# First-layer experts on gathered token blocks, with the second attention's first key stacks loaded in the same stage

## The chip, the cores and the metric

The kernel runs on one core of a Trainium2 chip. The metric is the device time of one execution in microseconds (us). Engines are named as in the profile: PE (TensorE matmul), PEld (its weight loads), DVE (VectorE), ACT (ScalarE), POOL (GpSimd), SP (SyncE, which here only issues DMAs; its rows are called SPq).

## The reference, cut to what matters

Four sequences of 256 tokens (1024 tokens, width 256) pass two layers, each a cross-attention and a mixture of experts. The change lies in the experts of the first layer, and touches what stands beside them. What they compute, for all 1024 rows `x` after a layer norm:

```python
topk_indices, topk_weights = _router(x, router_weight, e_bias)      # 2 of 16 experts per token
combine = zeros((T, 16)).at[arange(T)[:, None], topk_indices].add(topk_weights)
h1 = einsum('th,ehi->tei', x, w_up)                                 # 256 -> 128 per expert
a = relu2(h1) * combine[:, :, None]                                 # relu, squared
routed = einsum('tei,eih->th', a, w_down)                           # 128 -> 256
shared = relu2(x @ shared_up) @ shared_down                         # 256 -> 512 -> 256, all tokens
return routed + shared
```

The second attention has 16 heads of 16 over the same context; its queries come from the rows that this stage leaves, its keys only from the context.

## The kernel before

The program is a row of stages, and all engines meet between them: first attention (`prep_l0`, `attention` with `L0`), the first experts (`route_and_experts_l0`), the second attention (`load_first_units`, `attention` with `L1`), and the second layer's router, shared expert and routed experts (`route_shared_l1`, `routed_l1`). Tokens lie in 8 tiles of 128 rows; a half is 4 tiles. Every engine runs its own list of instructions in program order, and semaphores join them.

In `route_and_experts_l0` PE transposes the normed rows into `xT`, projects them on the router, and then runs the shared expert in 8 units (`hidden`, `outputs`), with one tile of the second attention's values (`values`) behind each. ACT rectifies a unit's hidden rows, POOL squares them (line 1131). Meanwhile DVE picks each token's two experts and writes the weights of all 16 to `comb` (lines 1256 to 1289).

The routed experts follow as a dense loop of 32 units `n` (16 experts times two halves): `routed_hidden(n)` multiplies an expert's up weights with all 512 rows of the half (line 1041), ACT rectifies, POOL squares (line 1141), `routed_outputs(n)` gives four tiles of outputs (line 1052), and DVE adds each to `xs`, times its weight, which is zero for most rows (line 1392). Expert weights (256 KB each) come through four slots of `f_w`, each loaded by SP when its unit is done (line 1427). Behind unit `n` each engine runs `keys(n)` and `queries(n)`: the second attention's keys, their norm and their split into three bf16 parts, and from unit 16 on the same for the queries of the first half, since `xs` of that half is then finished. SP writes the parts to the stacks in memory (`written`, line 233), and between its loads also fetches the second layer's first 12 experts (`load_weights`, line 1760).

The second attention begins with `load_first_units`: SP loads the key and query stacks of four units (line 469), keys first; the first scores (line 629) wait for both of unit 0. `LateQueries` makes the queries of the second half in that stage.

Of the kernel before, what the change touches and what calls it, by code (L numbers as in the profile page):

```python
# [210 lines left out]
KEYS_WRITTEN = (20, 21, 23, 24)  # L211
SPLIT_BANKS = (6, 7, 0, 1)
# [24 lines left out]
def prep_l0(nc, m, io, block, ctx):  # L237
# [158 lines left out]
    def _(pool):  # L396
        load_ones(pool, m, io, lay, m.ks0)
        nc.gpsimd.memset(m.v1[:], 0.0)
# [93 lines left out]
def attention(nc, m, lay, io, block, w_dram, b_dram, v_bias=None, late=None):  # L492
# [18 lines left out]
    with ExitStack() as ctx:  # L511
# [38 lines left out]
        def _(sp):  # L550
# [9 lines left out]
            for u in range(U):  # L560
                shift_rows(u, u % NBUF)
                if u == 0 and lay is L0:
                    for k in (4, 5):
                        load_side(sp, m, lay, ks, "k", loaded, k, k)
                        load_side(sp, m, lay, qs, "q", loaded, k, k)
                if u == 1 and late is not None:
# [345 lines left out]
WSLOTS = 4  # L912
GRP, GSZ = 4, 4


def route_and_experts_l0(nc, m, io):

    with ExitStack() as ctx:
# [3 lines left out]
        def sb(n, shape, dt=F32):  # L922
# [9 lines left out]
        hot, den = sb("hot", [2, NT, E0]), sb("den", [NT])  # L932
        ld, step, root_in, root_out, xn_ready, xt_ps, xt_ready, logit_ps, score_ready = (sem(n) for n in (
# [5 lines left out]
        UNITS0 = 2 * E0  # L939
        qh_xn, qh_turned, qh_copied, qh_ps, qh_cent, qh_squared, qh_summed, qh_scaled = (sem("qh_" + n) for n in (  # L940
            "xn", "turned", "copied", "ps", "cent", "squared", "summed", "scaled"))
        erelu, ehid = sb("erelu", [2, HT]), sb("ehid", [2, HT])
        e_up_ps, e_relu_done, e_hid_done, e_down_ps, e_added, comb_ready = (sem(n) for n in (
            "e_up_ps", "e_relu_done", "e_hid_done", "e_down_ps", "e_added", "comb_ready"))
        s_loaded = [sem(f"s_loaded{e}") for e in range(SH0)]
# [3 lines left out]
        hvar, hwork, sq = sb("hvar", [NT, H]), sb("hwork", [4, NT * H]), sb("sq", [2, D])  # L949
# [11 lines left out]
        def _(sp):  # L961
# [3 lines left out]
            sp.dma_start(later[:], io["later"].partition_broadcast(P)).then_inc(ld, 16)  # L965
            for e in range(SH0):
                sp.dma_start(sup[:, e, :, :].rearrange("p c n -> p (c n)"), io["L0_w"][E0 + e, :, 0:KD * I0]
                             ).then_inc(s_loaded[e], 16)
                sp.dma_start(sdown[:, e, :], io["L0_w"][E0 + e, :, KD * I0:KD * I0 + D]).then_inc(s_loaded[e], 16)
            for j in range(WSLOTS):  # L970
                load_expert_l0(sp, m, io, j, j)
# [20 lines left out]
        def _(pe):  # L992
# [106 lines left out]
            for n in range(UNITS0):  # L1099
                if n + 1 < UNITS0:  # L1100
                    routed_hidden(n + 1)
# [1374 lines left out]
```

## Time and profile before

| | us |
|---|---|
| median of 3 runs (lowest to highest) | 764.84 (762.67 to 765.81) |
| the profiled execution's own time | 768.52 |
| its span, first to last instruction | 766.6 |
| first experts' stage, to the first row of the next | 194.06 to 370.18 |
| of it the dense loop on PE | 244.37 to 368.05 |
| PE busy over the span | 646.2 (84%) |

The durations below are of the profiled execution, which lies 3.68 us above the median. Busy shares are means over stages with different limits, so each stage is read by itself: which engine is full there, and what ended the waits of the others. A matmul's record is longer than its place in the pipeline, so the cost of a matmul is read from where the next one starts.

### The profile page before, as it was taken

How to read it: one execution, taken by the hardware profiler on the slowest of the kernel's cores; microseconds unless marked ns; L12 is line 12 of the kernel's file. 1: busy time of each engine (PE TensorE's matmuls, PEld its weight loads, DVE VectorE, ACT ScalarE, POOL GpSimd, SP SyncE). 2: the span in 40 equal slices, each digit the busy share in tenths (PEclk: the TensorE clock that was granted, in tenths of full speed). 3: DMA queues.
4: the chain of work that ended last, by engine and by line, in shares of the span. 5: the costliest groups of instructions: out<-in, count | busy, mean ns of one | idle time of the engine just before them, and what ended most of it. 6: DMA issues, size and time to landing. Idle time of an engine off the chain costs nothing. (4 is left out here: it accounts for less than half of the span.)

```text
span 766.6 us, 12462 instructions
## 1 busy us (share of the span) xinstructions
PE 646.2 (84%) x4224; PEld 388.7 (51%) x4224; DVE 425.9 (56%) x1130; ACT 297.3 (39%) x552; POOL 259.2 (34%) x403
## 2 busy tenths in 40 slices
PE   1657988887799999999569999599999999999750
PEld 1542444444566666676335556365666555555330
DVE  4668788863330767967687564448982222222116
ACT  1332777785323122423036667342214232232110
POOL 5350011111135323313101333302258677777140
PEclk9895899998599999999779999759999999999875
DMA  3086122100600464553914310099001899999907
GB/s 116 1 277 197 45 64 64 45 2 1 175 0 1 127 182 151 166 179 97 240 32 126 85 45 2 12 276 245 4 12 36 236 290 276 271 269 279 266 32 274
DMA packets 82615, 99.59 MB, mean 130 GB/s; under 512 B 11610, under 2 KB 58049, under 8 KB 82547
## 3 DMA queue, kind: packets, MB, share of 16 engines
q1 hardware_dynamic: 74738, 86.53, 39.9%
q0 software_dynamic: 5600, 8.53, 4.3%
q10 hardware_dynamic: 2208, 3.67, 1.3%
q8 instruction: 36, 0.59, 0.3%
q14 instruction: 33, 0.26, 0.1%
HBM read 82.42 MB, written 21.63 MB: 136 GB/s over the span
## 5 line engine op out<-in xcount | busy, mean ns | idle before, releaser
L769 DVE TENSOR_REDUCE l_mx<-ps 128x2 f32<-128x512 f32 (+2 forms) x256 | 125.9, 550 | 46.7 <-PE ps L629 46.4
L857 ACT ACTIVATE l_prob<-ps 128x1024 f32<-128x1024 f32 x96 | 98.4, 1026 | 27.0 <-PE ps L659 26.8
L629 PE MATMUL ps<-l_ks,l_qs 48*128 48x256 bf16 (+1 forms) x384 | 73.1, 305 | 26.4 <-DMA l_qs<-l_q_stacks 13.2
L1392 DVE SCALAR_TENSOR_TENSOR xs<-ps,comb,xs 128x256 f32<-128x256 f32 x128 | 55.8, 482 | 59.5 <-PE ps L1052 59.4
L674 PE MATMUL ps<-l_prob,v 128*9 128x256 f32 (+1 forms) x768 | 71.4, 395 | 1.1 <-ACT l_prob L857 1.1
L2146 POOL DMA_INDIRECT y_rows<-r_sw,row x53 | 53.4, 1008 | 44.3 <-DVE r_sw L2287 33.6
L2280 DVE TENSOR_TENSOR r_hot<-r_hot,ps 128x352 f32<-128x352 f32 (+1 forms) x35 | 15.1, 432 | 95.1 <-ACT r_hot L2255 95.1
L1141 POOL TENSOR_TENSOR r_ehid<-r_erelu 128x512 f32<-128x512 f32 x32 | 35.5, 1109 | 83.6 <-ACT r_erelu L1245 83.5
L1790 POOL DMA_INDIRECT xg<-x_rows,r_empty x53 | 56.2, 1060 | 19.9 <-issue 10.5
L1052 PE MATMUL ps<-f_w,r_ehid 128*128 128x256 f32 x256 | 60.8, 381 | 0.2
L1041 PE MATMUL ps<-xT,f_w 128*128 128x512 f32 x128 | 60.0, 593 | 0.0
L629 PEld LDWEIGHTS ps<-l_ks,l_qs 48*128 48x128 bf16 (+1 forms) x384 | 30.1, 103 | 58.0 <-issue 21.8
L1052 PEld LDWEIGHTS ps<-f_w,r_ehid 128*128 128x128 f32 x256 | 48.5, 190 | 21.0 <-issue 13.9
L659 PE MATMUL ps<-l_qs,l_ks 50*128 50x256 bf16 (+1 forms) x384 | 57.6, 285 | 0.0
L597 POOL TENSOR_TENSOR attn<-rest,l_rec 128x32 f32<-128x32 f32 x64 | 14.4, 246 | 115.0 <-DVE l_rec L788 115.0
L597 POOL TENSOR_TENSOR l_ctxv<-rest,l_rec 128x64 f32<-128x64 f32 x64 | 17.6, 296 | 84.6 <-DVE l_rec L788 84.6
L2255 ACT ACTIVATE r_hot<-ps 128x352 f32<-128x352 f32 (+1 forms) x35 | 13.7, 392 | 79.8 <-PE ps L2184 79.8
L1874 PE MATMUL ps<-xT,r_sw 128*128 128x512 f32 x88 | 42.2, 621 | 0.0
L2287 DVE TENSOR_SCALAR r_sw<-ps,row_w 128x256 f32<-128x256 f32 x53 | 24.0, 481 | 30.1 <-PE ps L2205 30.1
L674 PEld LDWEIGHTS ps<-l_prob,v 128*9 128x9 f32 (+1 forms) x768 | 27.2, 99 | 23.4 <-issue 10.2
L2184 PE MATMUL ps<-ew,r_at_low 128*64 128x352 f32 (+1 forms) x304 | 38.3, 465 | 0.1
L2184 PE MATMUL ps<-ew13b,r_at_low 128*64 128x352 f32 (+1 forms) x240 | 33.3, 478 | 5.4 <-DMA ew2b<-in_L_w 5.4
(278 smaller groups left out, 1110.4 us busy)
## 6 DMA issues: line engine op xcount, KB each, us to landing
ew<-in_L_w SPq DMA_DIRECT2D x18, 704.0 KB, 8.1
ew13b<-in_L_w SPq DMA_DIRECT2D x12, 704.0 KB, 10.9
f_w<-in_L_w SPq DMA_DIRECT2D x32, 256.0 KB, 2.7
ew<-in_L_w SPq DMA_DIRECT2D x18, 384.0 KB, 9.8
ew2b<-in_L_w SPq DMA_DIRECT2D x12, 384.0 KB, 13.9
ew13b<-in_L_w SPq DMA_DIRECT2D x12, 352.0 KB, 13.1
l_k_stacks<-part SPq DMA_DIRECT2D x8, 384.0 KB, 3.3
l_ks<-l_k_stacks SPq DMA_DIRECT2D x32, 96.0 KB, 2.2
```

The costliest lines, as they stand in the source:

```text
L629: ins = nc.tensor.matmul(ps[:, score_bank(n) + k, qt * S:(qt + 1) * S], qs[row:row + R, u % NBUF, col, qt * P:(qt + 1) * P], ks[row:row + ...
L659: ins = nc.tensor.matmul(ps[:, 2 + 2 * (n % 2) + k, kt * S:(kt + 1) * S], ks[row:row + lay.krows, b, col, kt * P:(kt + 1) * P], qs[row:row ...
L674: ins = nc.tensor.matmul(ps[row:row + W, 6, (c % 2) * S:(c % 2 + 1) * S], v[:, n // UP // GR * QT + kt, head, :], prob[:, n % PROBS, k, kt ...
L769: ins = nc.vector.reduce_max(mx[:, u % 2, :, s, head], one[:, :, lo:hi], AX_X)
L857: nc.scalar.activation(prob[:, n % PROBS, :, :, :].rearrange("p h k q -> p (h k q)"), ps[:, 2 + 2 * (n % 2):4 + 2 * (n % 2), :].rearrange( ...
L1041: ins = nc.tensor.matmul(m.ps[:, n % 2, :], m.f0_up[:, n % WSLOTS, c, :], m.xT[:, c, half * HT:(half + 1) * HT], start=(c == 0), stop=(c = ...
L1052: nc.tensor.matmul(m.ps[:, 2 + t, 0:D], ehid[:, n % 2, t * P:(t + 1) * P], m.f0_down[:, n % WSLOTS, :], start=True, stop=True).then_inc(e_ ...
L1392: v.scalar_tensor_tensor(m.xs[:, i, :], m.ps[:, 2 + t, 0:D], m.comb[:, i, e:e + 1], m.xs[:, i, :], ALU.mult, ALU.add).then_inc(e_added, 1)
L1790: nc.gpsimd.indirect_dma_start(m.xg[:, b % XBUF, :], None, m.x_rows, bass.IndirectOffsetOnAxis(m.token[:, b:b + 1], 0), bounds_check=T - 1 ...
L1874: ins = nc.tensor.matmul(ps[:, 2 * (q % 2) + a, :], sw13[:, k, own], m.xT[:, k, h * TILES * P:(h + 1) * TILES * P], start=(k == 0), stop=( ...
L2146: nc.gpsimd.indirect_dma_start(m.y_rows, bass.IndirectOffsetOnAxis(m.row[:, b:b + 1], 0), yb[:, b % YBUF, :], None, bounds_check=ROWS - 1, ...
L2184: ins = nc.tensor.matmul(ps[row:row + n, spot(b), 0:2 * I1], xgT[:, spot(b), c * P + row:c * P + row + n], w13[:, s, c, :], start=(c == 0) ...
```

## The change

A token's row is now multiplied with its own two experts alone. `HBLOCKS` is 23 blocks of 128 rows for each half: one per expert, and 7 spare blocks for experts that more than 128 tokens of the half chose. 46 blocks (`NB0`) always run, full or not.

- **Router.** PE counts each token's rank within its expert (`ranks`, 28 small bf16 matmuls behind shared unit 1); DVE makes of it each token's two rows (`pick`), the experts of the spare blocks (`over`) and the two weights.
- **Rows out and back.** POOL scatters the normed rows to `x0_rows` in memory with 16 indirect DMAs. SP loads them as blocks, two blocks in one DMA (`load_x`), and stores each block's outputs to `y0_rows`. POOL gathers a half's outputs with 8 indirect DMAs when all 23 blocks are stored, and DVE adds them to `xs` (`combine`). The rows of `x0_rows` are zeroed before, by 12 DMAs in the first attention.
- **Block step.** 49 steps: PE runs `turn_x(b+2)`, `up(b+1)`, `down(b)`, then `keys(b)` and `queries(b-19)`; ACT runs `copy_x(b+2)`, `rectify(b+1)`, `copy_y(b)`; DVE runs `square(b+1)`. The shared expert's square moves from POOL to ACT.
- **Weights.** All 16 experts are loaded at the stage's start into the space of `ew13`, the spare blocks' experts through four slots of their own. `ew13` is filled in the second attention (`load_weights` with part 0), `ew2` in the second layer's router stage.
- **Key stacks.** They lie in the space of `ew2` and are loaded behind block 26 (`KEYS_LOADED`); `load_first_units` loads queries alone.

PE in the dense loop before, from unit 1 to unit 2 (`f_w` an expert's weights, `r_ehid` the squared hidden rows):

```order
L1041 MATMUL ps<-xT,f_w 128x512 [waits r0_e_relu_done,f0_loaded2]
L1041 MATMUL ps<-xT,f_w 128x512
L1052 MATMUL ps<-f_w,r_ehid 128x256 [waits r0_e_added,r0_e_hid_done]
L1052 MATMUL ps<-f_w,r_ehid 128x256 [waits r0_e_added] x3
L1041 MATMUL ps<-xT,f_w 128x512 [waits r0_e_relu_done,f0_loaded3]
```

PE at the same place now, steps 1 and 2 of the block loop (`k_tm` holds the loaded rows, `xT` a block's transposed rows, `ew` the experts' weights, `r_relu` the squares):

```order
L1148 MATMUL ps<-ident,k_tm 128x128 [waits r0_e_xt_done,r0_xb_ld1]
L1148 MATMUL ps<-ident,k_tm 128x128
L1168 MATMUL ps<-xT,ew 128x128 [waits r0_e_relu_done,r0_e_xt_done]
L1168 MATMUL ps<-xT,ew 128x128
L1176 MATMUL ps<-ew,r_relu 128x256 [waits r0_e_hid_done]
L1148 MATMUL ps<-ident,k_tm 128x128 [waits r0_e_xt_done,r0_xb_ld2]
```

Six matmuls of a unit have become five of a quarter or an eighth of the work, with waits on ACT, DVE and a row load in each step. SP at the stage's start before (`r_kw`, `r_vw` the second attention's key and value weights; the last of these loads, `r_vb`, is not shown):

```order
L969 DMA r_sdown<-in_L_w 128x256
L1427 DMA f_w<-in_L_w 128x512 x4
L1510 DMA r_kw<-in_L_wmain 128x256
L1510 DMA r_kw<-in_L_xattn_Wkv_dca 128x256
L1510 DMA r_kw<-in_L_bmain 128x256
```

and now:

```order
L1029 DMA r_sdown<-in_L_w 128x256
L1031 DMA ew<-in_L_w 128x512 x16
L1730 DMA r_kw<-in_L_wmain 128x256
L1730 DMA r_kw<-in_L_xattn_Wkv_dca 128x256
L1730 DMA r_kw<-in_L_bmain 128x256
```

Sixteen loads of 256 KB stand ahead of those weights instead of four. The core of the diff:

```diff
+OVER0 = (2 * HT - 1) // (P + 1)
+HBLOCKS = E0 + OVER0
+NB0 = 2 * HBLOCKS
+XB0, YB0, YG0 = NT, 4, NT
+QUERY_LAG = 19
+COMBINED = QUERY_LAG + 16 - TILES
+STEPS0 = max(NB0, QUERY_LAG + 30)
...
-            for j in range(WSLOTS):
-                load_expert_l0(sp, m, io, j, j)
+            for e in range(E0):
+                sp.dma_start(m.f0_base[:, e, :], io["L0_w"][e]).then_inc(m.f0_base_ld, 16)
             load_kv1(sp, m, io, kw, vw, pmask, vb, k_ld, k_small)
...
-            for n in range(UNITS0 - WSLOTS):
-                sp.wait_ge(e_down_ps, 4 * (n + 1))
-                load_expert_l0(sp, m, io, (n + WSLOTS) % E0, n % WSLOTS)
-                if n % 3 == 2 and n // 3 < PAIRS:
-                    load_weights(sp, m, io, n // 3 * 2)
-                if n in KEYS_WRITTEN:
-                    written(KEYS_WRITTEN.index(n))
+            for b in range(NB0):
+                sp.wait_ge(e_y_done, b + 1)
+                sp.dma_start(m.y0_rows[b // HBLOCKS][b % HBLOCKS * P:(b % HBLOCKS + 1) * P, :], yb[:, b % YB0, :]).then_inc(y0_sent[b % YB0], 16)
+                for pair in range(XB0 // 2, 2 * HPAIRS):
+                    if pair_end(pair - XB0 // 2) == b + 1:
+                        load_x(pair)
+                k = over_of(b)
+                if k is not None and k + WSLOTS < 2 * OVER0:
+                    load_over(k + WSLOTS)
+                if b in KEYS_WRITTEN:
+                    written(KEYS_WRITTEN.index(b))
+                if b == KEYS_LOADED:
+                    for a in range(SB):
+                        sp.wait_ge(part_dma[a], 16 * WRITES)
+                    for u in range(UNIT_BUFS[L1.name]):
+                        load_side(sp, m, L1, m.ks1, "k", m.loaded1, u, u)
...
+            turn_x(0)
+            turn_x(1)
+            up(0)
+            for b in range(STEPS0):
+                if b + 2 < NB0:
+                    turn_x(b + 2)
+                if b + 1 < NB0:
+                    up(b + 1)
+                if b < NB0:
+                    down(b)
+                keys(b)
+                queries(b - QUERY_LAG)
...
+            pool.wait_ge(picked_ready, 1)
+            for h in range(2):
+                for i in range(h * TILES, (h + 1) * TILES):
+                    for j in range(2):
+                        nc.gpsimd.indirect_dma_start(m.x0_rows[h], bass.IndirectOffsetOnAxis(pick[:, j, i:i + 1], 0),
+                                                     m.xn[:, i, :], None).then_inc(x0_sent[h], 16)
+                if h == 0:
+                    add_half(0)
+            add_half(1)
+            for h in range(2):
+                for j in range(YB0):
+                    own = len([b for b in range((h + 1) * HBLOCKS) if b % YB0 == j])
+                    pool.wait_ge(y0_sent[j], 16 * own)
+                for t in range(TILES):
+                    if h:
+                        pool.wait_ge(combined, t + 1)
+                    for j in range(2):
+                        nc.gpsimd.indirect_dma_start(yg[:, 2 * t + j, :], None, m.y0_rows[h], bass.IndirectOffsetOnAxis(
+                            pick[:, j, h * TILES + t:h * TILES + t + 1], 0)).then_inc(yg_ld[t], 16)
...
+            def copy_y(b):
+                act.wait_ge(e_down_ps, b + 1)
+                if b >= YB0:
+                    act.wait_ge(y0_sent[b % YB0], 16 * (b // YB0))
+                nc.scalar.copy(yb[:, b % YB0, :], ps[:, 4 + b % 2, 0:D]).then_inc(e_y_done, 1)
...
-        for a in range(SB):
-            sp.wait_ge(part_dma[a], 16 * WRITES)
-        load_side(sp, m, lay, m.ks1, "k", m.loaded1, 0, 0)
         for a in range(2):
             sp.wait_ge(part_dma[a], 2 * 16 * WRITES)
-        load_side(sp, m, lay, m.qs1, "q", m.loaded1, 0, 0)
-        for u in range(1, UNIT_BUFS[lay.name]):
-            load_side(sp, m, lay, m.ks1, "k", m.loaded1, u, u)
+        for u in range(UNIT_BUFS[lay.name]):
             load_side(sp, m, lay, m.qs1, "q", m.loaded1, u, u)
```

## Rows read from the trace of the kernel before

**Rows 1.** Windows by stage: us, length, busy of five engines, PE clock, DMA share, GB/s.

```profile
209.00:244.00 35.00, 35.00 (x120) 23.50 (x120) 8.72 (x49) 9.94 (x25) 13.66 (x28) 0.93 0.03 7
244.00:368.00 124.00, 123.84 (x459) 83.66 (x457) 88.44 (x207) 37.90 (x76) 38.27 (x36) 1.00 0.48 148
120.00:180.00 60.00, 52.74 (x599) 26.86 (x594) 44.60 (x108) 47.18 (x74) 7.08 (x32) 1.00 0.10 29
```

**Rows 2.** Groups by line, 194 to 370 us: busy, mean ns, idle before, releasers.

```profile
L1392 DVE SCALAR_TENSOR_TENSOR xs<-ps,comb,xs 128x256 f32<-128x256 f32 x128 | 55.8, 482 | 59.5 <-PE ps L1052 59.4
...
L1141 POOL TENSOR_TENSOR r_ehid<-r_erelu 128x512 f32<-128x512 f32 x32 | 35.5, 1109 | 83.6 <-ACT r_erelu L1245 83.5
...
L1245 ACT ACTIVATE r_erelu<-ps 128x512 f32<-128x512 f32 x32 | 19.0, 594 | 41.0 <-PE ps L1041 41.0
```

**Rows 3.** Timeline of PE in the loop: start us, us, line, count.

```profile
292.95 1.88 PE L1041 MATMUL ps<-xT,f_w 128*128 128x512 f32 x4
...
294.66 1.89 PE L1052 MATMUL ps<-f_w,r_ehid 128*128 128x256 f32 x8
...
296.39 1.88 PE L1041 MATMUL ps<-xT,f_w 128*128 128x512 f32 x4
...
354.61 1.04 PE L1449 MATMUL ps<-ident,q_tm 128*128 128x128 f32 x8
```

**Rows 4.** Groups by line, 194 to 370 us: ACT copy and activation, DVE square's shape.

```profile
L1166 ACT COPY r_ysh<-ps 128x256 f32<-128x256 f32 x8 | 2.4, 387 | 2.5 <-PE ps L1011 2.5
...
L1151 ACT ACTIVATE r_score<-ps 128x128 f32<-128x128 f32 x1 | 0.3, 277 | 5.8 <-PE ps L197 5.8
L1256 DVE TENSOR_TENSOR r_biased<-r_score,r_bias 128x128 f32<-128x128 f32 x1 | 0.3, 294 | 10.4 <-ACT r_score L1151 10.4
```

**Rows 5.** Timeline, start of the stage and shared expert: start us, us, idle before.

```profile
199.77 1.85 SPq L1427 DMA_DIRECT2D f_w<-in_L_w  x4
...
209.27 2.58 POOL L1118 COPY v<-r_pmask 128x16 f32<-128x16 f32 x16 [14.18 <-DMA r_vb<-in_L_vb_T]
...
215.34 0.60 ACT L1172 ACTIVATE r_relu<-ps 128x512 f32<-128x512 f32 x1 [2.02 <-PE ps L1001]
...
218.96 1.89 PE L1011 MATMUL ps<-r_sdown,r_hid 128*128 128x256 f32 x8
```

**Rows 6.** Windows, as rows 1: the loads of the stage's start.

```profile
198.00:206.00 8.00, 7.18 (x31) 5.65 (x31) 1.08 (x4) 3.89 (x8) 0.00 (x0) 0.50 0.92 288
```

**Rows 7.** Timeline of POOL's indirect DMAs in the second layer.

```profile
570.80 1.97 POOL L1790 DMA_INDIRECT xg<-x_rows,r_empty  x1 [0.30 <-issue]
...
590.20 1.01 POOL L1790 DMA_INDIRECT xg<-x_rows,r_empty  x1 [0.30 <-PE ps L2172]
...
744.95 0.98 POOL L2146 DMA_INDIRECT y_rows<-r_sw,row  x1 [0.30 <-issue]
747.58 0.09 POOL L2162 MEMSET r_hot<- 1x1 f32 x1 [1.65 <-DMA y_rows<-r_sw,row]
```

**Rows 8.** DMA issues: KB each, median us to landing.

```profile
l_ks<-l_k_stacks SPq DMA_DIRECT2D x8, 384.0 KB, 4.8
l_qs<-l_q_stacks SPq DMA_DIRECT2D x8, 384.0 KB, 5.7
...
out_x<-xs SPq DMA_DIRECT2D x8, 128.0 KB, 2.9
```

**Rows 9.** Tile out_x: landing times of its 128 KB stores.

```profile
DMA to landing us min/median/max: 1.7/2.9/6.9
```

**Rows 10.** Timeline, end of the stage and start of the second attention.

```profile
364.09 3.96 PE L1052 MATMUL ps<-f_w,r_ehid 128*128 128x256 f32 x16
...
370.18 0.38 DVE L157 BATCH_NORM_AGGREGATE mv<-bn 128x2 f32<-128x6 f32 x4 [0.30 <-PEq L918]
...
370.68 0.49 SPq L469 DMA_DIRECT2D l_qs<-l_q_stacks  x1
...
377.14 1.03 PE L629 MATMUL ps<-l_ks,l_qs 96*128 96x256 bf16 x4 [9.09 <-DMA l_qs<-l_q_stacks]
```

More of the change, by code:

```diff
@@ L211 @@
 KEYS_WRITTEN = (20, 21, 23, 24)
+KEYS_LOADED = 26
 SPLIT_BANKS = (6, 7, 0, 1)
@@ L1055, in keys, with down @@
+            def down(b):
+                pe.wait_ge(e_hid_done, b + 1)
+                if b >= 2:
+                    pe.wait_ge(e_y_done, b - 1)
+                nc.tensor.matmul(ps[:, 4 + b % 2, 0:D], hT[:, b % 4, :], expert(b)[:, KD * I0:KD * I0 + D],
+                                 start=True, stop=True).then_inc(e_down_ps, 1)
             def keys(n):
@@ new lines, in _ @@
+            slot, far = (t[:].rearrange("p (h i) e -> p h i e", h=2) for t in (score, biased))
+            many = more[:].rearrange("p i g h -> p (i g h)")[:, 0:6 * E0].rearrange("p (h e n) -> p h e n", h=2, n=3)
+            link(v.tensor_copy(count[:].rearrange("p h e -> p (h e)"), ps[:, 6, NT * E0:(NT + 2) * E0]))
+            for h in range(2):
+                ins = v.tensor_tensor(many[:, h, :, :], bcast(count[:, h, :], 2, 3), bcast(marks[:], 1, E0), ALU.is_gt)
+            link(ins)
+            link(v.tensor_reduce(extra[:], many, AX_X, ALU.add))
@@ new lines, in _ @@
+            link(ins)
+            link(v.tensor_tensor(masked[:], score[:], biased[:], ALU.add))
+            at = [t[:].rearrange("p i g h -> p i (g h)") for t in (more, same)]
+            for j in range(2):
+                ins = v.tensor_tensor(at[j], hot[:, j, :, :], masked[:], ALU.mult)
+            link(ins)
+            for j in range(2):
+                ins = v.tensor_reduce(picked[:, j, :], at[j], AX_X, ALU.add)
+            link(ins)
+            v.tensor_copy(pick[:], picked[:]).then_inc(picked_ready, 1)
@@ new lines, in _, with square @@
+            for j in range(2):
+                ins = v.tensor_tensor(at[j], hot[:, j, :, :], comb[:], ALU.mult)
+            link(ins)
+            for j in range(2):
+                ins = v.tensor_reduce(weight[:, j, :], at[j], AX_X, ALU.add)
+            link(ins)
+            def square(b):
+                dve.wait_ge(e_relu_done, b + 1)
+                if b >= 4:
+                    dve.wait_ge(e_down_ps, b - 3)
+                v.tensor_tensor(hT[:, b % 4, :], reluT[:, b % 4, :], reluT[:, b % 4, :], ALU.mult).then_inc(e_hid_done, 1)
@@ new lines, in combine @@
+            def combine(i):
+                half, t = i // TILES, i % TILES
+                if i == 0:
+                    dve.wait_ge(added, NT)
+                dve.wait_ge(yg_ld[t], 32 * (half + 1))
+                for j in range(2):
+                    ins = v.scalar_tensor_tensor(m.xs[:, i, :], yg[:, 2 * t + j, :], weight[:, j, i:i + 1], m.xs[:, i, :],
+                                                 ALU.mult, ALU.add)
+                    if j == 0:
+                        link(ins)
+                ins.then_inc(combined, 1)
@@ L2459, in host_layout @@
     io["starts"] = slot_starts()
+    e, half = np.arange(E0), np.arange(2)[:, None]
+    io["starts0"] = np.stack([P * e + 0 * half, P * (E0 - 1 - e) + 0 * half]).astype(np.float32)
+    io["keep0"] = np.broadcast_to((e > 0).astype(np.float32), (2, E0)).copy()
+    io["marks0"] = np.arange(1, 4, dtype=np.float32) * P
     io["upper"] = np.triu(np.ones((P, P), np.float32), 1)
```

287 lines of the change are left out of this document (201 added, 86 removed).

## The prediction

> **What bounds the kernel now.** I read the windows by stage first, since the change lies in one stage. In the dense loop PE is busy 123.84 of 124 us at the full clock (1.00, the level of 2.4 GHz), while DVE has 88, ACT 38, POOL 38 and the DMA engines 0.48 of their time [rows 1]. The groups by line agree: DVE, POOL and ACT sat idle 59, 84 and 41 us before their rows of the loop, and what ended that was PE, or an engine that had itself waited for PE [rows 2]. So this stage is a PE stage, and DVE's 128 additions and POOL's 32 squares, however long, end on time. The timeline gives the price of a unit: from 292.95 to 296.39, 3.44 us [rows 3]. 32 units are 110.1 of the loop's 123.7 us (244.37 to 368.05); the other 13.6 us are PE's keys and queries, which the change keeps.
>
> **The block loop, PE's part.** Eight records of 256 columns take 1.73 us (294.66 to 296.39), 0.216 each, and eight of 128 columns 1.04 us with the tail of the last, so about 0.11 each [rows 3]. A block costs two transposes (4 records of 128 columns, 0.44), two up matmuls (0.44) and one down matmul (2 records of 256 columns, 0.43): 1.31 us. 46 blocks are 60.3 us against 110.1; with 13.6 us of keys and queries PE needs 73.9 us, 50 us less than now. That is the gain on offer. The rest of the sum is what takes its place.
>
> **Late at the start.** The second attention's weights now stand behind 16 expert loads on SP's queue, not four. The queue is full there: 288 GB/s in the window 198 to 206 us [rows 6]. Twelve more loads of 262 KB are 3.1 MB, 10.9 us; four new constants cost SP four issues at 0.46 us (four took 1.85 [rows 5]), 1.8 us. POOL's fill of `v1`, which waited 14.18 us for the last of these loads, starts at 209.27 now [rows 5], so about 222, and ends 2.6 us later at 224.6. ACT waits for it ahead of the second rectify (now 215.34), squares by itself (0.6 us), and PE's second output block, now at 218.96 [rows 5], starts near 225.7: 6.7 us late. The rank matmuls add about 1 us. PE leaves the shared expert at 252.1 instead of 244.4. The router does not add to this: ranks at 230, some 15 DVE rows at about 0.3 us [rows 4] to 235, eight scatters at 1.31 (1.01 and 0.30 idle) to 245.5, landing at most 2.6 after the start of the last (744.95 to 747.58) [rows 7], row loads by 251. It is late by nothing as long as that 1 us of slack holds. The first `down` then needs two row copies, a rectify, a square and the copies of the shared outputs ahead of them on ACT, 3.8 us: 255.9. Bounds of this term: +1 us (had the weights come in time) to +11.
>
> The Trainium skill, "DMA: Bandwidth & Descriptors", section "Queues, rings and completion order", says that each engine's issuing queue has one ring on each DMA engine and that descriptors are consumed in ring order; by that rule loads behind the experts cannot overtake them, and the trace agrees as far as the wait of 14.18 us behind a full queue goes [rows 5, 6].
>
> **Lost time in the loop.** ACT has two copies of 128x256 and a rectify of 128x128 for each block, 0.39 + 0.39 + 0.28 = 1.05 us, DVE one square of 0.29 [rows 4]; both fit under PE's 1.31, and the lags of one or two steps cover the hops. Three places do not fit.
> - Steps 0 to 2: DVE centres the key and query weights between squares that PE needs one step later; about 2 us.
> - Steps 13 to 34: the DMA engines. 22 stores and 22 blocks loaded (5.8 MB), seven spare experts (1.8), four key parts written six times 128 KB (3.1), four key stacks of 393 KB read back (1.6) and the first half's gathers (1.0) are 13.3 MB. At 288 GB/s [rows 6] that is 46 us; PE has 22 times 1.31 and four splits of 0.9, 32.3 us. A store's buffer is taken again four steps later and rows are loaded some five steps ahead, so a backlog soon reaches ACT and PE: 14 us lost. SP itself, which also stops at block 26 until the key parts have landed, is inside that.
> - Steps 35 to 45: the queries. Dense units of 3.44 us hid the hops between engines; steps of 1.31 do not. In two steps PE waits behind its own `down` for ACT's copy of the store and then of the turned rows (about 1.4 us each), and in three steps DVE holds the next square behind ACT's squares and root (about 4 us together): 7 us, an estimate from the durations in rows 4.
> So from the first to the last `down` 73.9 - 1.7 (transposes of the query split, which come after it) + 2 + 14 + 7 = 95 us: the last ends near 351. Bounds: 76 (nothing lost) and 112 (below).
>
> **The tail.** Today 368.05 to 370.18 closes the stage. Now the last block must be copied (0.6), stored and landed (2.9 for 128 KB [rows 8]), then gathered: eight indirect DMAs, the last starting 9.2 us after the first, landing 2.6 later [rows 7], then DVE's two additions at 0.48 [rows 2] and the statistics of four tiles. That is 17 us; the query parts are written in the same stretch and share the DMA engines, so I take 19 (14 to 25). The query split and its writes, some 16 us from the last `down`, are hidden by this. The stage ends at 370: no earlier than today.
>
> **Elsewhere.** The zeroing writes 6 MB in the first attention, where the DMA share is 0.10 [rows 1]; the early experts' `w13` goes to the second attention and `w2` to the router stage of the second layer, each well ahead of its use: 0, at most +3. The first scores wait until 377.14 for unit 0's queries, issued at 370.68 behind its keys [rows 10], where a stack of 384 KB takes 4.8 to 5.7 us to land among eight [rows 8]. With the keys there already, the queries are first on an empty queue: about 374, -3 us (0 to -4). This carries on, since the late queries' chain starts behind these scores.
>
> **The sum.** Start +7.7 and 3.8 of fill, loop and tail in place of 123.7 and 2.1: the stage ends 0 us earlier; -3 in the second attention. 768.52 - 3 = 765.5 for a profiled execution; the median of before lies 3.7 lower, so 762.
>
> **Rivals.**
> - A: the loop runs closer to PE. For it: DMA engines can move writes and reads beside each other, buffers let a backlog pass, and 14 + 7 us of loss is mostly inference. If half of it is gone, 10 us: 752; if the start is on time too, 745. Against it: 13.3 MB in 32 us would be 412 GB/s, where a full queue moved 288 [rows 6].
> - B: the store ring decides, and the kernel is slower. ACT's `copy_y` waits for the store four blocks earlier, so a step cannot be shorter than a quarter of copy, issue and landing. With 1.1 us for the first two, it binds as soon as a store lands later than 4.1 us (4 x 1.31 - 1.1). 128 KB stores take 1.7 to 6.9 us, median 2.9 [rows 9]. At 6.9 each step is 2.0 us, 46 of them 92, with the queries' 7, the start's 2 and some key work 108 to 112 us, and the time is 775 to 779. Stores stand in one queue with loads of 262 KB, which speaks for it; most stretches of the loop are not crowded, which speaks against every step being so.
> - C: the early key stacks bring nothing, because the first scores wait for the queries' own writes, which end with the tail: 765.
> - D: POOL's indirect DMAs are slowed. One took 1.97 us while DVE was in large additions [rows 7]. If the tail's eight go at 2.27, that is +7.7: 770. DVE is idle for most of the tail, so it is unlikely. The Trainium skill, "DMA: Bandwidth & Descriptors", section "SWDGE vs HWDGE vs iDMA", says that GpSimd writes such descriptors to rings in SBUF, from which DVE's two-port mode locks it out, while DMAs issued by SP are immune; the long row is what that rule would give, though no row isolates it.
>
> **How the numbers follow.** The forecast has 0.40, A 0.30, B 0.17, C 0.06, D 0.07. 0.5% of 764.84 is 3.8 us, about what a measurement of this kernel can tell from no change: faster is under 761.0, slower above 768.7. The forecast's own 757 to 767 gives 0.15 faster, 0.21 same, 0.04 slower; A 0.28 and 0.02; B all slower; C same; D 0.07 slower. Sum: 0.43, 0.29, 0.28. The range runs from 748 (A without its extreme) to 778 (B with it), and the likeliest case's own is 757 to 767.
>
> **What would show it.** Right or wrong by step: the fill of `v1` near 222 us and the second shared square near 225; PE's last shared row near 252; the last `down` near 351, with PE busy about three quarters of the block loop and the loss lying in steps 13 to 34 under a DMA share above 0.9; waits of `copy_y` for stores (B) or of PE for row loads there; gathers ending some 17 us behind the last `down`; the first scores some 4 us behind the stage's end. The forecast is wrong if the DMA share in the middle stays near today's 0.48, if the clock in the loop falls to its lower level of 1.2 GHz (a PE step is then 2.6 us), or if the start is late for the router's sake and not the weights'.

## The result: slower, 787.65 us instead of 765.33

| | before | after |
|---|---|---|
| median (lowest to highest) | 765.33 us (762.67 to 770.26, 4 runs) | 787.65 us (786.17 to 789.65, 4 runs) |
| ratio to before, 95% interval | | 1.0325 (1.0277 to 1.0373) |
| the profiled execution, its span | 768.52, 766.6 | 787.64, 785.8 |

The prediction was 762 us with a range of 748 to 778. The changed kernel is 22.3 us slower and lies outside the range. In the two profiled executions the spans differ by 19.2 us; the profiled run of before lies 3.2 us above its median, that of after on it. So the spans explain 19.2 us, and the rest is the distance of that run from its median.

The first thing to make of two traces is a table by stretch, cut at instructions that both have. For the changed kernel "start" ends at PE's first `down`, for the kernel before at the first matmul of the dense loop; the loop ends before with PE's last `down` record, after where block 45's `down` starts, 0.7 us ahead of its end:

| stretch | before, us | after, us | difference |
|---|---|---|---|
| start of the stage to the loop | 50.31 | 58.90 | +8.6 |
| loop, first to last `down` | 123.68 | 105.60 | -18.1 |
| tail, to the stage's end | 2.13 | 18.75 | +16.6 |
| to the second attention's first scores | 6.96 | 4.33 | -2.6 |
| to its last projection | 112.42 | 123.20 | +10.8 |
| to the router's first transposes | 8.58 | 10.29 | +1.7 |
| to the end | 268.5 | 270.6 | +2.1 |

The stage that was changed costs 7.1 us more than before. Behind it the largest loss, 10.8 us, is in the second attention, which computes what it did before.

### The profile page after: what moved, and what is told of

It is laid out like the page before. It is cut to its first block and busy times, and to the rows that moved or that the text cites. A ratio compares the mean times of both kernels' runs of the same rounds, so it can differ in the third digit from the quotient of the medians.

```text
span 785.8 us, 12907 instructions
## 1 busy us (share of the span) xinstructions
PE 608.5 (77%) x4236; PEld 372.4 (47%) x4236; DVE 396.4 (50%) x1093; ACT 324.6 (41%) x666; POOL 246.2 (31%) x395
## 5 line engine op out<-in xcount | busy, mean ns | idle before, releaser
L778 DVE TENSOR_REDUCE l_mx<-ps 128x2 f32<-128x512 f32 (+2 forms) x256 | 126.0, 549 | 55.8 <-PE ps L638 55.4
L683 PE MATMUL ps<-l_prob,v 128*9 128x256 f32 (+1 forms) x768 | 73.8, 402 | 1.1 <-ACT l_prob L866 1.1
L2001 POOL DMA_INDIRECT xg<-x_rows,r_empty x53 | 55.3, 1043 | 19.8 <-issue 10.5
L638 PE MATMUL ps<-l_ks,l_qs 48*128 48x256 bf16 x256 | 46.7, 302 | 13.6 <-DVE l_mx L778 9.5
L1500 DVE TENSOR_TENSOR r_relu<-r_relu 128x128 f32<-128x128 f32 x46 | 13.7, 300 | 73.1 <-ACT r_relu L1396 73.1
L638 PE MATMUL ps<-ew,l_qs 96*128 96x256 bf16 x128 | 27.3, 318 | 28.2 <-DMA l_qs<-l_q_stacks 17.5
L1275 POOL DMA_INDIRECT r_yg<-y_rows,r_pick x16 | 15.4, 960 | 98.4 <-DMA y_rows<-r_hid 94.1
L668 PE MATMUL ps<-l_qs,l_ks 50*128 50x256 bf16 x256 | 37.1, 285 | 0.0
L638 PEld LDWEIGHTS ps<-l_ks,l_qs 48*128 48x128 bf16 x256 | 16.8, 100 | 39.1 <-issue 18.9
L2198 POOL TENSOR_TENSOR r_hid<-r_hid,r_lin 128x512 f32<-128x512 f32 (+1 forms) x12 | 16.4, 1364 | 54.7 <-ACT r_lin L2161 54.7
L2418 PE MATMUL ps<-ew,r_hot 88*64 88x256 f32 (+1 forms) x304 | 32.8, 419 | 0.7 <-ACT r_hot L2461 0.7
```

What stands on the lines that cost most here:

```text
L638: ins = nc.tensor.matmul(ps[:, score_bank(n) + k, qt * S:(qt + 1) * S], qs[row:row + R, u % NBUF, col, qt * P:(qt + 1) * P], ks[row:row + ...
L668: ins = nc.tensor.matmul(ps[:, 2 + 2 * (n % 2) + k, kt * S:(kt + 1) * S], ks[row:row + lay.krows, b, col, kt * P:(kt + 1) * P], qs[row:row ...
L683: ins = nc.tensor.matmul(ps[row:row + W, 6, (c % 2) * S:(c % 2 + 1) * S], v[:, n // UP // GR * QT + kt, head, :], prob[:, n % PROBS, k, kt ...
L778: ins = nc.vector.reduce_max(mx[:, u % 2, :, s, head], one[:, :, lo:hi], AX_X)
L2001: nc.gpsimd.indirect_dma_start(m.xg[:, b % XBUF, :], None, m.x_rows, bass.IndirectOffsetOnAxis(m.token[:, b:b + 1], 0), bounds_check=T - 1 ...
L2418: ins = nc.tensor.matmul(out_ps[spot(b)][row:row + n, :], hidT[:, spot(b), c * P + row:c * P + row + n], w2[0:HC, s, c, :], start=(c == 0) ...
```

## The profile after

The windows of the changed stage (columns as in rows 1): blocks 0 to 13, 13 to 34, 34 to 45, and the tail.

```profile
253.00:278.50 25.50, 21.96 (x128) 19.10 (x129) 14.59 (x35) 14.66 (x47) 4.96 (x6) 0.93 0.38 124
278.50:335.70 57.20, 34.30 (x186) 27.99 (x186) 19.72 (x53) 27.44 (x82) 7.63 (x8) 0.83 0.82 235
335.70:358.60 22.90, 17.97 (x107) 14.56 (x105) 10.87 (x37) 11.95 (x38) 0.00 (x0) 0.97 0.44 130
358.60:377.30 18.70, 2.64 (x10) 1.86 (x10) 10.25 (x21) 3.49 (x6) 7.73 (x8) 0.57 0.45 150
```

PE, busy for 123.84 of 124 us in the dense loop [rows 1], is busy for 74.2 of 105.6 us here (21.96, 34.30 and 17.97 added). The work that was to go is gone, and waiting stands in its place, most of it in blocks 13 to 34. There no engine is full, and the DMA share is 0.82.

What PE and ACT waited for in the loop (line, releaser: us in total, times, longest):

```profile
PE ps L1148 <- DMA k_tm<-x_rows: 16.1, 5, 7.7
ACT r_hid L1390 <- DMA y_rows<-r_hid: 14.0, 4, 8.0
PE ps L1176 <- DVE r_relu L1500: 9.7, 6, 3.0
PE ps L1168 <- DMA f_over<-in_L_w: 3.2, 2, 2.5
```

PE waits for loaded rows (`turn_x`), and ACT's `copy_y` for stores, both behind the DMAs. The longest wait of each ends at 331 to 332. SP's timeline ahead of it:

```profile
317.30 0.46 SPq L1049 DMA_DIRECT2D k_tm<-x_rows  x1
319.57 4.09 SPq L470 DMA_DIRECT2D ew<-l_k_stacks  x4
323.71 2.50 SPq L1066 DMA_DIRECT2D y_rows<-r_hid  x2
326.25 0.46 SPq L1049 DMA_DIRECT2D k_tm<-x_rows  x1
```

SP stands still from 317.76 to 319.57 until the key parts have landed, then issues the four key stacks for 4.09 us; stores and row loads go out behind them. PE's row:

```profile
332.25 0.69 PE L1148 MATMUL ps<-ident,k_tm 128*128 128x128 f32 x2 [7.72 <-DMA k_tm<-x_rows]
```

The second attention, SP's timeline of one unit:

```profile
420.35 0.44 SPq L1971 DMA_DIRECT2D ew<-in_L_w  x1
420.90 0.40 SPq L470 DMA_DIRECT2D l_qs<-l_q_stacks  x1
421.35 0.54 SPq L470 DMA_DIRECT2D ew<-l_k_stacks  x1
```

A load of 704 KB of the second layer's weights, `w13`, stands right ahead of the two stacks that the next unit's scores wait for. The packets show the order. From 421.0 to 423.5 nearly all are the load's, over 2 KB; from 424.0 to 427.0 nearly all are the stacks', under 2 KB:

```profile
DMA packets 201, 0.54 MB, mean 216 GB/s; under 512 B 7, under 2 KB 10, under 8 KB 201
...
DMA packets 1534, 0.77 MB, mean 258 GB/s; under 512 B 35, under 2 KB 1531, under 8 KB 1534
```

Two stacks of 384 KB are 0.77 MB. PE waits 3.13 us for them, until 427.98. PE's waits for key stacks in the second attention, after:

```profile
PE ps L638 <- DMA ew<-l_k_stacks: 10.0, 4, 3.2
```

and before:

```profile
PE ps L629 <- DMA l_ks<-l_k_stacks: 3.0, 3, 1.7
```

That is 7.0 of the 10.8 us. The windows of that stretch, first scores to last projection, have the rest in PE's own column. Before:

```profile
377.14:489.56 112.42, 98.40 (x667) 58.75 (x667) 69.00 (x219) 65.00 (x115) 27.78 (x96) 0.89 0.25 65
```

and after:

```profile
381.68:504.88 123.20, 101.96 (x666) 59.55 (x667) 69.20 (x219) 65.13 (x115) 27.77 (x96) 0.87 0.32 85
```

The same matmuls take 3.6 us longer at a granted clock of 0.87 instead of 0.89 of full speed.

## The experiments

All times are medians, with the ratio to the kernel before and its 95% interval; the kernel before, measured beside the runs, had medians of 764.46 to 765.88 us. The stretches, from the profiled execution of each (start to first `down`; blocks 0 to 13, 13 to 34, 34 to 45; tail; to the first scores; to the last projection), in us:

| kernel | start | 0-13 | 13-34 | 34-45 | tail | scores | projection |
|---|---|---|---|---|---|---|---|
| after | 58.9 | 25.5 | 57.2 | 22.9 | 18.8 | 4.3 | 123.2 |
| `w13` in the router stage | 60.9 | 25.5 | 55.8 | 22.2 | 19.1 | 4.6 | 112.7 |
| key stacks loaded at the attention | 61.0 | 25.5 | 48.8 | 22.9 | 18.9 | 5.9 | 121.7 |
| attention weights first | 53.4 | 25.6 | 56.4 | 23.2 | 19.2 | 4.0 | 123.6 |
| key traffic late | 59.0 | 25.6 | 38.8 | 25.8 | 21.0 | 4.6 | 123.9 |
| three together | 54.2 | 25.6 | 36.0 | 29.0 | 20.7 | 4.6 | 112.9 |
| eight store buffers | 61.5 | 25.6 | 56.5 | 22.2 | 19.3 | 4.0 | 125.2 |
| three, and DVE early | 53.6 | 20.1 | 37.4 | 25.8 | 20.8 | 3.7 | 112.1 |
| that, queries later | 54.5 | 20.1 | 36.3 | 24.2 | 22.1 | 4.3 | 113.4 |
| that (queries as they were), key stacks at the attention | 53.4 | 20.1 | 37.9 | 26.3 | 19.2 | 5.7 | 112.9 |

**1. `w13` back in the router stage.**

```diff
-                if lay is L1 and 1 <= u <= EARLY // 2:
-                    load_weights(sp, m, io, 2 * (u - 1), 0)
...
-            load_weights(sp, m, io, 2 * q, 1)
+            load_weights(sp, m, io, 2 * q)
```

> The early experts' first weights (six loads of 704 KB) are taken out of the second attention and stand in the second layer's router stage again, each ahead of its second weights. Theory: in the second attention each of these loads stands on SP's queue right ahead of the query and key stacks of a unit, and PE waits 10.0 us for key stacks there instead of 3.0; from the first scores to the last projection it takes 123.2 us (381.68 to 504.88) instead of 112.4 (377.14 to 489.56). Without them: waits near 3 us, 112 to 115 us for that stretch, a time of 777 to 780. Rival: the stacks are late because they are written and read in the shared space, or because the chip runs the attention at a lower clock: then the stretch stays near 123 us and the time near 787. Second rival: the router stage has no room for the loads, and the routed experts wait for them: 787 or more.

Measured 777.12 us, 1.0147 (1.0097 to 1.0197). The stretch to the last projection is 112.7 us, as in the kernel before. PE's waits there:

```profile
PE ps L636 <- DMA ew<-l_k_stacks: 4.0, 4, 1.1
```

So six loads in the second attention cost 10.5 us (four of them stand right ahead of key stacks), and neither the shared space of the key stacks nor the clock by itself did. The stacks have the same space here, and the clock in that stretch was higher (0.91) once the waits were gone. That it is the loads' place in the queue is read from the packets above; no run kept them in that stage behind the stacks. The router stage had room for the loads: from its first transposes to the end took 267.1 us. The Trainium skill, "DMA: Bandwidth & Descriptors", section "Queues, rings and completion order", says that descriptors of one issuing queue are consumed in ring order; the 10.0 us that became 4.0 agree with it.

**2. Key stacks loaded at the second attention's start**, as in the kernel before, keys ahead of queries.

```diff
-                if b == KEYS_LOADED:
-                    for a in range(SB):
-                        sp.wait_ge(part_dma[a], 16 * WRITES)
-                    for u in range(UNIT_BUFS[L1.name]):
-                        load_side(sp, m, L1, m.ks1, "k", m.loaded1, u, u)
```

> The four key stacks are loaded at the second attention's start again, keys ahead of queries, and not behind block 26. Theory: in the block loop SP stands still at block 26 for the key parts, issues 1.6 MB, and stores and row loads queue behind them; PE's wait of 7.7 us for rows at 332 goes, the last down comes 6 to 9 us earlier (358.60 now), the first scores come 2 to 3 us later behind the stage's end, and the time is 781 to 784. Rival: the loss in steps 13 to 34 is one of latency from store to buffer to row load and shows elsewhere when this wait goes: last down within 2 us of 358.6, time 788 to 791.

Measured 779.52 us, 1.0167 (1.0119 to 1.0215), a little better than expected. Blocks 13 to 34 are 8.4 us shorter (57.2 to 48.8); the first scores come 1.6 us later behind the stage's end. Where it stood, the early load of the key stacks cost five times what it brought.

**3. The second attention's weights ahead of the experts.**

```diff
+            load_kv1(sp, m, io, kw, vw, pmask, vb, k_ld, k_small)
             for e in range(E0):
                 sp.dma_start(m.f0_base[:, e, :], io["L0_w"][e]).then_inc(m.f0_base_ld, 16)
-            load_kv1(sp, m, io, kw, vw, pmask, vb, k_ld, k_small)
```

> The second attention's key and value weights are loaded ahead of the 16 experts and not behind them. Theory: the start is late for these weights alone (POOL's fill at 220.18 instead of 209.27): the fill starts near 209, PE leaves the shared expert near 246 instead of 250.1, and the first down is 4 to 5 us earlier, at 248 to 249. If the loop's middle is bound by what its DMAs move from step 13 on, these 4 us are kept, for the middle starts earlier as well: time 783. Rival: the router sets the start, as the rows are scattered by 245 and loaded by 248: first down at 251 or later, time 786 to 788.

Measured 781.18 us, 1.0184 (1.0123 to 1.0245). The first `down` is 5.5 us earlier in its stage (53.4 instead of 58.9), a little more than expected, and the router sets nothing there. In the profiles whose start no edit touches it takes 58.9 to 61.5 us, in those with this edit 53.4 to 54.5. POOL's fill starts 15.3 us behind the stage's start, 190.69, as in the kernel before (15.2), and not 26.1:

```profile
205.93 2.41 POOL L1249 COPY v<-r_pmask 128x16 f32<-128x16 f32 x16 [11.61 <-DMA r_vb<-in_L_vb_T]
```

Blocks 13 to 34 stay at 56.4 us: they start earlier and last as long, so the gain is kept.

**4. Key traffic late**: the parts written behind blocks 35 to 38, the stacks loaded behind the last block.

```diff
-KEYS_WRITTEN = (20, 21, 23, 24)
-KEYS_LOADED = 26
+KEYS_WRITTEN = (35, 36, 37, 38)
+KEYS_LOADED = 45
```

> The key parts are written to their stacks behind blocks 35 to 38 instead of 20 to 24, and the key stacks are loaded behind the last block's store instead of block 26. Theory: steps 13 to 34 move 13.6 MB in 57.2 us (235 GB/s) and are bound by that; 4.7 MB less make them 38 to 46 us, and steps 35 to 45 get longer by at most the 3.1 MB moved there (up to 6 us); the last down comes 8 to 16 us earlier, the tail grows by 0 to 5 us, time 775 to 782. Rival: the store ring and the row loads set these steps by their latency, which is there without the key traffic too: last down less than 4 us earlier, and with the loads in the tail the time is 786 to 792.

Measured 769.63 us, 1.0041 (1.0000 to 1.0082): 18.0 us less by the medians, for two lines, and better than the 775 to 782 expected. The windows of the same four stretches:

```profile
250.60:276.15 25.55, 21.84 (x129) 18.92 (x129) 14.64 (x35) 14.72 (x47) 4.97 (x6) 0.93 0.39 125
276.15:314.95 38.80, 31.82 (x186) 26.08 (x185) 18.80 (x51) 27.13 (x82) 7.64 (x8) 0.87 0.68 204
314.95:340.76 25.81, 18.05 (x107) 13.94 (x105) 11.84 (x39) 12.32 (x39) 0.00 (x0) 1.00 0.83 266
340.76:361.75 20.99, 2.63 (x10) 1.86 (x10) 10.28 (x21) 3.49 (x6) 8.10 (x9) 0.53 0.84 211
```

The middle is 18.4 us shorter; what the 4.7 MB cost where they went is 2.9 us in blocks 34 to 45 and 2.2 us in the tail. From the stage's start to the last projection the profile is 12.0 us shorter than that of the changed kernel. The rest of the 17.7 us between their spans lies ahead of the stage and behind the last projection, in code that is the same, and these parts differ by as much between profiles of other runs; so 12 us are shown where the edit acts. The waits of the loop:

```profile
PE ps L1148 <- DMA k_tm<-x_rows: 2.9, 2, 1.7
...
ACT r_hid L1390 <- DMA y_rows<-r_hid: 1.7, 3, 1.1
```

Both fell together, from 16.1 and 14.0 us. With run 2, 8.4 of the 18.4 us belong to the stacks that are read and, by subtraction, 10.0 to the parts that are written; no run moved the parts alone.

**5. The three together** (1, 3 and 4).

> Three single changes together: the early experts' first weights in the second layer's router stage, the second attention's weights ahead of the experts, and the key parts written behind blocks 35 to 38 with the key stacks loaded behind the last block. Alone they gave 10.5, 6.5 and 18.0 us. Theory: they act in three different places (second attention, start of the stage, steps 13 to 34 of the loop), so they add: 787.65 - 35 = 753, with 750 to 757 as bounds; first down near 242, first scores to last projection near 112.7 us. Rival: two of them take away the same waiting (the start and the middle both end in what the DMAs move, or the loads in the router stage collide with what now comes earlier): 758 to 768.

Measured 751.75 us, 0.9813 (0.9772 to 0.9854): 35.9 us faster than the changed kernel, where the three alone sum to 35.0. They add, as they lie in three places: from the stage's start to the last projection the three profiles are 10.1, 5.4 and 12.0 us shorter, 27.5 in all, and this one is 27.8 (its execution lies 7.1 us above the median). The kernel is now faster than the one before.

**6. Eight store buffers** in the changed kernel; four semaphores were merged with others to make room for theirs.

```diff
-XB0, YB0, YG0 = NT, 4, NT
+XB0, YB0, YG0 = NT, 8, NT
...
-        relu, hid = sb("relu", [2, HT]), sb("hid", [2, HT])
+        relu, yb = sb("relu", [2, HT]), sb("hid", [YB0, D])
+        ysh = yb[:, 4:8, :]
+        hid = yb[:, 0:4, :].rearrange("p (a j) d -> p a (j d)", a=2)
...
+                if b == 4:
+                    act.wait_ge(added, NT)
```

> Only the store ring is changed: eight buffers for block outputs instead of four, the other four in the space of the shared outputs' copies. Theory: ACT's waits for stores in the middle (14.0 us in four of them) are the DMA backlog seen from ACT, and PE waits there for loaded rows (16.1 us) behind the same queue; with a longer ring the rows are still late, the last down moves by less than 3 us from 358.6, time 785 to 789. Rival (the ring decides, case B of the prediction): steps 13 to 34 get shorter by most of ACT's 14 us, the last down comes 8 us earlier or more, time 774 to 780.

Measured 787.66 us, 1.0279 (1.0222 to 1.0337): no change. ACT no longer waits for stores at all, and PE waits for rows as before:

```profile
PE ps L1149 <- DMA k_tm<-x_rows: 16.2, 5, 6.1
```

So ACT's 14.0 us were the same backlog seen from another engine, and the prediction's rival B falls.

**7. The three, and DVE's early work.** The centring of the weights and the clearing of semaphores stand ahead of the loop; the root of the keys' variance is begun in step 12, taken by ACT in step 13 and finished in step 14.

```diff
+            dve.wait_ge(k_ld, 7 * 16)
+            centre_heads(nc, link, kw[:], ksums).then_inc(kw_ready, 1)
+            dve.wait_ge(q_ld, 32)
+            dve.wait_ge(kw_ready, 1)
+            link(centre_heads(nc, link, m.qw[:], ksums))
+            m.clear_sems(dve)
             square(0)
...
-                if n == 13:
+                if n == 12:
...
+                if n == 14:
+                    rsqrt_finish(nc, dve, chain, roots, hroot_out, 1)
```

> The three changes together, and two moves on DVE: the centring of the key and query weights and the clearing of semaphores stand ahead of the block loop instead of in its steps 0 to 2, and the root of the keys' variance is begun a step earlier on DVE and ACT and finished in step 14, so that DVE doesn't wait for ACT in between. Theory: PE waits 2.30 and 1.25 us for squares in steps 2 and 4 and 2.98 us in step 15, and its clock falls to 0.50 behind the first of these waits; without them the loop is 5 to 9 us shorter than with the three changes alone. Rival: the rows come back from memory late enough that PE waits for them instead, or the time is given back in the middle: less than 2 us.

Measured 745.64 us, 0.9707 (0.9653 to 0.9762): the fastest, 6.1 us below run 5 and 2.9% below the kernel before. The windows of the loop, cut at blocks 13 and 34:

```profile
247.53:267.62 20.09, 19.89 (x129) 17.77 (x129) 10.11 (x29) 14.79 (x47) 4.85 (x6) 1.00 0.57 177
267.62:305.00 37.38, 29.50 (x186) 24.03 (x185) 18.66 (x51) 26.87 (x82) 7.87 (x8) 0.95 0.72 218
305.00:330.82 25.82, 18.23 (x107) 14.02 (x105) 11.86 (x39) 12.36 (x39) 0.00 (x0) 1.00 0.81 256
```

In blocks 0 to 13 PE is busy for 19.89 of 20.09 us at a clock of 1.00, where the same blocks took 25.55 us at 0.93. The first scores lie 161.4 us behind the stage's start, against 187.6 in the changed kernel and 183.1 in the kernel before.

**8. Queries five steps later** (`QUERY_LAG` 24) on top of run 7.

> The kernel of the run before, with the queries 24 steps behind the blocks instead of 19. Theory: steps 35 to 45 take 23 us for 11 blocks because DVE's and ACT's query work stands between them; five steps later most of it falls into the tail, where PE is idle for 18 us: the last down comes 4 to 7 us earlier and the stage's end with it, but the query stacks are written 0 to 3 us earlier only, so that the first scores gain 1 to 5 us. Rival: the query chain becomes what ends last, and the first scores come no earlier or later: time the same or up to 5 us more.

Measured 747.57 us, 0.9765 (0.9696 to 0.9835): no difference that this measurement can tell from run 7. The loop is 2.7 us shorter (80.6 against 83.3), less than expected, and the tail and the way to the first scores are 1.8 us longer.

**9. DVE's instructions shifted**, on top of run 7.

```diff
+            for i in range(24):
+                v.memset(hwork[0:1, 3, i:i + 1], 0.0)
             square(0)
```

> The kernel with the three changes and DVE's early work, and 24 one-element writes to an unused row on DVE at a place where it is idle for 14 us. Theory: in all kernels with the changed stage, DVE starts its last two additions of the second attention 6.50 us after the row before, 1.5 us later than in the kernel before (from the last projection to the router's first transposes 10.04 to 10.30 us instead of 8.58), with one packet of the instruction queue beside it: it waits there for its own instructions. Moved by 24 instructions, the place where a new piece is fetched falls elsewhere, and the stretch is 8.5 to 8.9 us. Rival: something else in that stretch is slower by 1.5 us: it stays at 10.0 to 10.3. The time moves by 1.5 us at most either way.

Ratio 0.9725 (0.9640 to 0.9810), which this measurement can't tell from run 7. It asks for the 1.7 us between the last projection and the router. DVE's row there in the kernel before:

```profile
492.45 0.42 DVE L801 TENSOR_TENSOR xs<-xs,ps 128x256 f32<-128x256 f32 x1 [4.89 <-PE ps L197]
```

in the changed kernel:

```profile
509.63 0.42 DVE L810 TENSOR_TENSOR xs<-xs,ps 128x256 f32<-128x256 f32 x1 [6.50 <-issue]
```

and with the shift:

```profile
470.57 0.42 DVE L808 TENSOR_TENSOR xs<-xs,ps 128x256 f32<-128x256 f32 x1 [6.50 <-PE ps L197]
```

The 6.50 us stay to the hundredth, the stretch takes 10.0 us as the rival expected, and the theory that DVE waits for its own instructions falls. The trace has what DVE does in that time, though the timeline leaves it out: it clears semaphores (`clear_sems`, line 108). Before and after:

```profile
L108 DVEq EVENT_SEMAPHORE_RANGE_CLEAR  x58: 54/54/54, 487.6 to 492.3; - x58
...
L108 DVEq EVENT_SEMAPHORE_RANGE_CLEAR  x73: 54/54/54, 503.2 to 509.5; - x73
```

The addition starts when the last one is done. They are semaphores that the stages up to there have used, and the changed kernel has 15 more of them to clear here. At one every 0.083 us that is 1.25 us, and one step of 0.44 us between two clears brings it to the 1.6. All ten runs clear 73 here, so no run takes them away; it is read from the trace alone.

**10. Key stacks at the second attention's start**, on top of run 7, with their parts still written behind blocks 35 to 38.

> The kernel with the three changes and DVE's early work, with the key stacks loaded at the second attention's start, as in the kernel before, and not behind the last block (their parts are still written behind blocks 35 to 38). It asks what the early load of the key stacks brings by itself. Theory: behind the last block the loads stand in the way of the last gathers (the tail is 20.8 us with them, 18.8 in the kernel as changed), and the first scores come 3.7 us behind the stage's end instead of 5.9: the two cancel, time within 1.5 us of the run with early loads (745.6). Rival: the early load is worth its 2 to 3 us, the tail is long for another reason: 748 to 749.

Measured 751.37 us, 0.9820 (0.9775 to 0.9866), outside what either the theory or the rival expected. By the medians alone the early load would be worth 5.7 us. By the stretches of the two profiled executions it is not: the tail is 1.6 us shorter and the first scores come 2.0 us later behind the stage's end, so 0.4 us in favour of the early load. What separates the two profiles is the last stretch, behind the router's first transposes, with 273.1 us against 267.7, in code that is the same. That stretch took 267.1 to 272.9 us in the profiles of runs 1 to 9, without an order that follows the edits. Whether it is chance here as well, one profile doesn't tell; the places that the edit touches say under 1 us.

## Why the prediction was wrong, step by step

- **PE bounds the dense loop, and its work falls by 50 us.** 123.5 us busy became 74.2, and 73.9 were predicted, but the agreement is luck: a block's price was too high. PE's timeline from the `down` of block 11 to that of block 12, after:

```profile
276.29 0.60 PE L1176 MATMUL ps<-ew,r_relu 128*128 128x256 f32 x2
276.73 0.38 PE L1148 MATMUL ps<-ident,k_tm 128*128 128x128 f32 x2
276.95 0.61 PE L1168 MATMUL ps<-xT,ew 128*128 128x128 f32 x4
277.39 0.64 PE L1176 MATMUL ps<-ew,r_relu 128*128 128x256 f32 x2
```

  They start 1.10 us apart, not 1.31. The two transposes (L1148) are two records, where two matmuls of the same shape (L1168) are four, so they take 0.22 us and not 0.44. 46 blocks at 0.21 us less are 9.7 us. Matmuls at a lower granted clock (0.83 in blocks 13 to 34) gave most of that back: in run 7, at 0.95 to 1.00, PE is busy in the loop for 67.6 us. So the prediction's sign that the clock might fall came in part.
- **Start.** The mechanism was right and its size nearly: the fill of `v1` started at 220.18 (222 predicted), PE left the shared expert at 250.08 (252.1), and the first `down` came at 253.00 (255.9). Run 3 showed that it is these weights, and that their order is worth 5.5 us there.
- **Blocks 0 to 13.** 2 us were allowed for DVE's early work; run 7 shows 5.5. The waits are 2.30 and 1.25 us, the first behind the centring, the second behind the clearing of 52 semaphores in step 2 (259.8 to 264.1), which the sum left out. Behind the first the granted clock is 0.50 for about 3 us, the lower level of 1.2 GHz, with PE busy all the time.
- **Blocks 13 to 34: the mis-sized term of the loop.** The DMAs moved 13.45 MB, where 13.3 were predicted, and that took 57.2 us and not 46. The stretch, cut at 290:

```profile
278.50:290.00 11.50, 7.99 (x55) 6.45 (x55) 6.83 (x16) 8.04 (x24) 0.00 (x0) 1.00 0.43 128
290.00:335.70 45.70, 26.31 (x134) 21.54 (x133) 12.89 (x37) 19.40 (x60) 7.63 (x8) 0.79 0.91 262
```

  The sum divided all bytes by one rate, as if the DMA engines had work from the first step on. In the first 11.5 us they moved 1.5 MB at a share of 0.43, and PE waited 2.98 us for DVE in step 15. 12.0 MB came behind that, at a share of 0.91 (the prediction's sign was above 0.9) and 262 GB/s. At the 288 of [rows 6] the two parts would take 5.1 and 41.6 us: an estimated 6.4 us were lost in the first and 4.1 in the second. In the second, two windows, with the gathers of the first half and the key parts' writes, and with the key stacks' reads:

```profile
315.00:320.00 5.00, 2.85 (x12) 2.57 (x13) 0.29 (x1) 1.02 (x3) 3.37 (x4) 0.68 1.05 363
...
325.00:330.00 5.00, 0.00 (x0) 0.00 (x0) 0.00 (x0) 0.00 (x0) 0.00 (x0) 0.70 1.18 196
```

  The DMA engines were busy throughout both, and moved 363 GB/s in one and 196 in the other, in which every other engine stood still. Packets under 2 KB don't explain the difference: they are 1418 of 1545 in the first and 1795 of 1796 in the second, and 1430 of 1943 in the window of [rows 6]. The packets of the second are about half as large on the mean (0.98 MB in all, against 1.82), but in the second attention the stacks' reads moved at 258 GB/s, so what makes them slow here is not shown. Runs 2 and 4 show that the key traffic alone is worth 18.4 us in this stretch, so the direction was right: the DMA traffic decides, not the ring of stores (run 6).
- **Blocks 34 to 45 and the tail.** Of the sum's 95 us for the loop, 46 are the middle's and 49 are left for blocks 0 to 13 and 34 to 45; measured are 25.5 and 22.9, 48.4 together. That is near by luck too, since the first of them lost 3.5 us more than allowed. For the tail 19 were predicted and 18.75 measured. POOL's gathers ran at a cadence of 1.25 us, and rival D didn't come.
- **The stage's end**: 370 predicted, 377.35 measured: the middle's 11 us, less 3 at the start and 1 in the rest.
- **The first scores**: 4 us behind the stage's end predicted, 4.33 measured.
- **Elsewhere: the step that failed.** It read "the early experts' `w13` goes to the second attention and `w2` to the router stage of the second layer, each well ahead of its use: 0, at most +3". They are ahead of their use, and the price is 10.5 us all the same (run 1). Without it the time would be 777.1, inside the range; without the middle's 11 us it would be inside as well. It took both. The prediction asked when the moved load is needed, and not what is queued behind it. It had priced just this for the weights at the stage's start, where 16 loads went ahead of others on SP's queue, and didn't look for it in the stage to which the loads moved.
- **The rivals.** A (closer to PE) and B (the store ring) fell; B's time of 775 to 779 was nearest, for a wrong reason. C (the early key stacks bring nothing, because the first scores wait for the queries' writes) fell in its reason, as the first scores come 2.6 us sooner behind the stage's end, and was too kind: run 2 shows that the stacks cost 6.8 us net where they stood.

What stays open: the 196 GB/s of the key stacks' reads; the 2.1 us behind the router, which lie within what that stretch differs by from profile to profile (267.1 to 273.1); and the part of run 4's gain that lies outside the stretches it touches.

## What to carry to other kernels

A load that is moved to where there is time for it must be followed down its queue: name the transfer that stands right behind it, and who waits for that one. Here six loads that nobody waited for cost 10.5 us, and two constants that say behind which block the keys are written and loaded cost 18 by the medians, 12 of them in the stretches they touch. When a loop loses its bound, price its transfers where they lie and not as one sum over the loop: here 12.0 of 13.45 MB fell into the last 45.7 of 57.2 us. Look at short waits too (2.30 us here), since one can cost almost its length again through PE's clock, and at work that the timeline doesn't list, such as the clearing of semaphores.

## What the runs showed of the hardware

- A wait of 2.30 us by PE in step 2 (until 257.76) was followed by matmuls at the lower clock. The windows of after (columns as in rows 1):

```profile
257.00:258.00 1.00, 0.24 (x1) 0.24 (x2) 1.00 (x2) 0.00 (x0) 1.00 (x2) 1.00 0.65 223
...
260.00:261.00 1.00, 1.00 (x3) 0.75 (x3) 0.11 (x1) 0.28 (x1) 0.00 (x0) 0.50 0.12 40
```

  Without that wait and the 1.25 us two steps on, the same 13 blocks took 20.1 us instead of 25.5, more than the waits' own 3.6.
- DMA engines at a share above 1 (as the view counts it) moved 196 GB/s in one stretch of 5 us and 363 GB/s in another of the same loop.
- Transfers that SP issued behind a load of 704 KB had their packets run behind the load's, from 424.0 on, though issued at 420.90 and 421.35; without that load ahead of them, issued at 419.06 and 419.48, they ran from 420.0 on.
- DVE clears a semaphore every 0.083 us: 58 took 4.81 us in the kernel before, 52 took 4.32 us in step 2 of the changed kernel. The timeline shows that time as idle, put down to "issue" or to an engine that was done before.
